# Counting and placing a graph's edges per block of source nodes: from broadcast rows with a scan to one-hot products with the edge on the partition

## The reference

```python
xt = jnp.einsum('nd,rde->rne', x, W)
agg = jax.ops.segment_sum(xt[rel, src], dst, num_segments=x.shape[0])
x = jax.nn.relu(agg + x @ SW + b)                     # twice
...
scores = jnp.einsum('ehd,ehd->eh', q[src], k[tgt]) / np.sqrt(HD) + (curv @ Wc + bc)
p = jnp.exp(scores - segment_max(scores, tgt)[tgt])
probs = p / segment_sum(p, tgt)[tgt]
out = jnp.zeros_like(x).at[src].add((probs[:, :, None] * v[tgt]).reshape(E, -1))
```

## Time and profile before

| | us |
|---|---|
| median of 3 runs | 9961.1 |
| lowest, highest | 9957.0, 10004.2 |
| the profiled execution, its own time | 10026.0 |
| its span | 10024.0 |
| POOL busy over the span | 6599.2 (66%) |
| DVE busy | 6480.5 (65%) |
| PE busy | 6317.1 (63%) |
| ACT busy | 2755.1 (27%) |

### The profile page before, as it was taken

One profiled execution on the slowest core, in us unless ns is written; L12 is line 12 of the kernel. 1 busy time (PEld: TensorE's weight loads), 2 busy tenths in 40 slices (PEclk: granted clock), 3 DMA queues, 4 the chain that ended last, 5 costly groups with the idle time before them and its releaser, 6 DMA issues. The chain is left out here.

```text
span 10024.0 us, 168284 instructions
## 1 busy us (share of the span) xinstructions
PE 6317.1 (63%) x28252; PEld 5567.6 (56%) x28253; DVE 6480.5 (65%) x17072; ACT 2755.1 (27%) x6953; POOL 6599.2 (66%) x6718
## 2 busy tenths in 40 slices
PE   0444444444676777767568888888735666666666
PEld 0233333333466666666448888888724565655555
DVE  6254444444566777766568888888864666666655
ACT  0100000000222222322135555555413333333301
POOL 1177777777377777777337777777647777777710
PEclk9755555555755555555565555555556777788757
DMA  1722222222322222222235555555424666666631
GB/s 29 216 62 62 62 62 62 62 62 62 140 58 55 61 60 60 61 55 59 57 100 137 137 137 137 137 137 137 117 60 117 147 150 149 146 151 151 150 91 30
DMA packets 1093415, 984.20 MB, mean 98 GB/s; under 512 B 224876, under 2 KB 970796, under 8 KB 1093243
## 3 DMA queue, kind: packets, MB, share of 16 engines
q0 software_dynamic: 214240, 442.60, 16.0%
q1 hardware_dynamic: 699363, 407.53, 15.4%
q10 hardware_dynamic: 179712, 133.04, 6.8%
HBM read 791.54 MB, written 210.74 MB: 100 GB/s over the span
## 5 line engine op out<-in xcount | busy, mean ns | idle before, releaser
L651 POOL DMA_INDIRECT stage_msg<-xt,stage_index x3328 | 3286.6, 988 | 1397.2 <-issue 1044.1
L673 PE MATMUL stage_ps_agg<-stage_hot,stage_msg 128*128 128x128 f32 x6656 | 1714.8, 439 | 1925.3 <-DMA stage_msg<-xt,stage_index 1761.0
L673 PEld LDWEIGHTS stage_ps_agg<-stage_hot,stage_msg 128*128 128x128 f32 x6656 | 1481.8, 328 | 2071.9 <-DMA stage_msg<-xt,stage_index 968.7
L1086 POOL DMA_INDIRECT big<-q,stage_index x1664 | 1587.3, 954 | 756.7 <-issue 488.4
L1474 POOL DMA_INDIRECT slots<-big,stage_index x1664 | 1681.3, 1010 | 530.8 <-issue 445.9
L746 DVE TENSOR_TENSOR big<-big,stage_ps_agg 128x128 f32 x3328 | 955.0, 287 | 1496.2 <-PE stage_ps_agg L673 1138.3
L620 ACT ACTIVATE stage_index<-big 128x4 int32 (+1 forms) x832 | 170.2, 205 | 2911.0 <-PE stage_ps_agg L673 2901.2
L1528 PE MATMUL stage_ps_sums<-stage_hot,big 128*128 128x128 f32 x4160 | 800.4, 361 | 182.0 <-DVE big L1646 174.1
L1518 PE MATMUL stage_ps_val<-nodes_a,big 128*128 x3328 | 665.1, 361 | 312.6 <-ACT big L1432 289.2
L1528 PEld LDWEIGHTS stage_ps_sums<-stage_hot,big 128*128 128x128 f32 x4160 | 728.8, 267 | 234.2 <-DVE big L1646 181.0
L1161 PE MATMUL stage_ps_key<-nodes_a,big 128*128 x3328 | 794.9, 414 | 0.0
(11 more groups left out here) (253 smaller groups left out, 8661.2 us busy)
## 6 DMA issues: line engine op xcount, KB each, us to landing
big<-slots SPq DMA_DIRECT2D x2080, 66.0 KB
big<-in_edge_attr_dram SPq DMA_DIRECT2D x1664, 64.0 KB
stage_trow<-targets ACTq DMA_DIRECT2D x832, 128.0 KB
xt<-big SPq DMA_DIRECT2D x26, 2048.0 KB, 6.6
stage_msg<-xt,stage_index POOLq DMA_INDIRECT x3328
stage_lanes<-buckets SPq DMA_DIRECT2D x832, 49.0 KB
big<-q,stage_index POOLq DMA_INDIRECT x1664
slots<-big,stage_index POOLq DMA_INDIRECT x1664
```

What stands on the lines that cost most here:

```text
L651: pool.indirect_dma_start(msg[q][:, j, :], None, xt, bass.IndirectOffsetOnAxis(ap=index[q][:, j:j + 1], axis=0))\
L673: last = nc.tensor.matmul(ps[q % 2][:, j, :], msg[q][:, j, :], hot[q % 2][:, j, :], start=True, stop=True)
L1086: pool.indirect_dma_start(qrow[q][:, j * D:(j + 1) * D], None, d["q"], bass.IndirectOffsetOnAxis(ap=index[q][:, j:j + 1], axis=0))\
```

## The change

- `prepare_edges` no longer makes `buckets`. Behind the transposes DVE makes `block` (source >> 7) from the transposed `source`, with the edge on the partition, and keeps it in SBUF in half precision.
- The broadcast rows, their DMAs on SP and the eight copies of the mark table go. `score` and `scatter` read the marks from `tile_marks` with the head as a dimension of stride zero.
- Both runs: DVE makes `block_hot`, a one-hot of 4 x 49 columns on 128 partitions, half precision, for group x+1, directly behind L723.
- First run: PE sums `block_hot` over the partitions and the four tiles by four half-precision products with one column of ones; ACT copies the result to `counts`, four groups later.
- Second run: DVE scales an identity by `begin` (`base`, 49 x 49). PE adds up in PSUM, for every edge and block, `begin` plus the earlier tiles' edges of the block plus the earlier edges of the tile: one single-precision product (196 columns) and four in half precision (147, 98, 49 and 196 columns). DVE multiplies that by `block_hot` and reduces over the blocks into `slot_of`. Scan, both ACT passes, ACT's copy and the four single-column products go.

```diff
         link(nc.vector.tensor_scalar(target[:, :, :], target[:, :, :], -1.0, None, ALU.add))
 
-        link(nc.vector.tensor_scalar(bucket, srow, 7, None, ALU.arith_shift_right))
-        link(nc.vector.tensor_copy(bucket16[:, :, :], bucket))
         link(nc.vector.tensor_scalar(penalty[:, :, :], valid[:, :, :], BIG, -BIG, ALU.mult, ALU.add))
...
+        v.wait_ge(s_cp, 2 * len(CH))
+        link(nc.vector.tensor_copy(block_i, t["source"][:, :]))
+        link(nc.vector.tensor_scalar(block_i, block_i, 7, None, ALU.arith_shift_right))
+        link(nc.vector.tensor_copy(t["block"][:, :], block_i))
...
+    CONST = 1 if first else 3
     block = m.stack.enter_context(nc.Block())
     xt = d["xt"].rearrange("n (r e) -> (n r) e", r=R)
 
-    @block.sync
-    def _(sp):
-
-        def group(x):
-            q = x.slot()
-            if x.live(-SLOTS):
-                sp.wait_ge(s_counted if first else s_own, x.at(-SLOTS) + 1)
-            sp.dma_start(lanes[q][:, :], d["buckets"][bass.ds(x.at() * (G * P), G * P)].partition_broadcast(W))\
-                .then_inc(s_lanes[q], 16)
-
-        if first:
-            for h in range(H):
-                sp.dma_start(d["marks"].rearrange("(k h) e -> k h e", h=H)[:, h, :], d["tile_marks"])\
-                    .then_inc(s_mk, 16)
-        walk(sp, group, 0, 0)
-        if first:
-            sp.wait_ge(s_mk, 16 * H)
-
...
+            if first and x.live(-SLOTS):
+                act.wait_ge(s_met, x.at(-SLOTS) + 1)
+                nc.scalar.activation(t["counts"][:, bass.ds(x.at(-SLOTS), 1)], ps_met[x.slot(-SLOTS, 2)][0:W, 0:1],
+                                     ACT.Copy).then_inc(s_counted, 1)
+
+        walk(act, group, 0, SLOTS if first else 0)
+        if first:
+            act.wait_ge(s_counted, GROUPS)
...
         def group(x):
             if x.live():
-                q = x.slot()
+                q, h = x.slot(), x.slot(0, 2)
                 pe.wait_ge(s_hot, x.at() + 1)
                 pe.wait_ge(s_read, x.at() + 1)
                 pe.wait_ge(s_msg[q], x.turn() * (16 * G) + (16 * G + at[q]))
                 for j in range(G):
-                    last = nc.tensor.matmul(ps[q % 2][:, j, :], msg[q][:, j, :], hot[q % 2][:, j, :],
+                    last = nc.tensor.matmul(ps[h][:, j, :], msg[q][:, j, :], hot[h][:, j, :],
                                             start=True, stop=True)
                 last.then_inc(s_freed, 1)
-            if not first and x.live(-2):
-
-                h = x.slot(-2, 2)
-                pe.wait_ge(s_pick, x.at(-2) + 1)
-                if x.live(-4):
-                    pe.wait_ge(s_kept, x.at(-4) + 1)
-                for j in range(G):
-                    last = nc.tensor.matmul(ps_slot[h][:, j:j + 1], pick[h][:, j * P:(j + 1) * P], one[:, :],
-                                            start=True, stop=True)
-                last.then_inc(s_slot, 1)
-
-        walk(pe, group, 0, 0 if first else 2)
+                pe.wait_ge(s_block_hot, x.at() + 1)
+                if first:
+                    if x.live(-2):
+                        pe.wait_ge(s_counted, x.at(-2) + 1)
+                    for j in range(G):
+                        last = nc.tensor.matmul(ps_met[h][0:W, 0:1], block_hot[h][:, j, :], ones16[:, 0:1],
+                                                start=(j == 0), stop=(j == G - 1))
+                    last.then_inc(s_met, 1)
+                else:
+                    pe.wait_ge(s_base, x.at() + 1)
+                    if x.live(-2):
+                        pe.wait_ge(s_pick, x.at(-2) + 1)
+                    rank = ps_rank[h][:, 0:G * W].rearrange("p (j w) -> p j w", w=W)
+                    nc.tensor.matmul(rank, ones[:, 0:P], base[h][:, :].unsqueeze(1).to_broadcast([W, G, W]),
+                                     start=True, stop=False)
+                    for j in range(G - 1):
+                        nc.tensor.matmul(rank[:, j + 1:G, :], ones16[:, :],
+                                         block_hot[h][:, j, :].unsqueeze(1).to_broadcast([P, G - 1 - j, W]),
+                                         start=False, stop=False)
+                    nc.tensor.matmul(rank, earlier[:, :], block_hot[h][:, :, :], start=False, stop=True)\
+                        .then_inc(s_rank, 1)
+
+        walk(pe, group, 0, 0)
 
     @block.vector
     def _(v):
         v.sem_inc(s_read, 2)
+        nc.vector.memset(ones16[:, :], 1.0).then_inc(s_const, 1)
         if not first:
...
         def group(x):
             if x.live(1):
+                h = x.slot(1, 2)
+                here = bass.ds(x.at(1) * G, G)
 
                 v.wait_ge(s_freed, x.at(1) + SLOTS - 1)
                 nc.vector.tensor_tensor(
-                    hot[x.slot(1, 2)][:, :, :], t["iota16"][:, :].unsqueeze(1).to_broadcast([P, G, P]),
-                    t["target"][:, bass.ds(x.at(1) * G, G)].unsqueeze(2).to_broadcast([P, G, P]),
-                    ALU.is_equal).then_inc(s_hot, 1)
-            if x.live():
-                h, q = x.slot(0, 2), x.slot()
-                if first:
-                    v.wait_ge(s_lanes[q], x.turn() * 16 + 16)
-                    if x.live(-1):
-                        v.wait_ge(s_counted, x.at())
-                    nc.vector.tensor_scalar(met[h][:, :], lanes[q][:, :], t["lane"][0:W, :], 0.0, ALU.is_equal,
-                                            ALU.add, accum_out=t["counts"][:, bass.ds(x.at(), 1)])\
-                        .then_inc(s_counted, 1)
...
-                else:
-                    v.wait_ge(s_own, x.at() + 1)
-                    if x.live(-2):
-                        v.wait_ge(s_pick, x.at(-2) + 1)
-                    nc.vector.tensor_tensor_scan(run[h][:, :], ones[:, :], own[h][:, :],
-                                                 begin[:, bass.ds(x.at(), 1)], ALU.mult, ALU.add).then_inc(s_run, 1)
+                    hot[h][:, :, :], t["iota16"][:, :].unsqueeze(1).to_broadcast([P, G, P]),
+                    t["target"][:, here].unsqueeze(2).to_broadcast([P, G, P]), ALU.is_equal).then_inc(s_hot, 1)
+                if x.live(-1):
+                    v.wait_ge(s_met if first else s_rank, x.at(-1) + 1)
+                    if not first:
+                        v.wait_ge(s_pick, x.at(-1) + 1)
+                nc.vector.tensor_tensor(
+                    block_hot[h][:, :, :], t["iota16"][:, 0:W].unsqueeze(1).to_broadcast([P, G, W]),
+                    t["block"][:, here].unsqueeze(2).to_broadcast([P, G, W]), ALU.is_equal).then_inc(s_block_hot, 1)
+                if not first:
+                    nc.vector.tensor_scalar(base[h][:, :], t["ident"][0:W, 0:W], begin[:, bass.ds(x.at(1), 1)], None,
+                                            ALU.mult).then_inc(s_base, 1)
+            if x.live():
                 w = offsets(nc, mybir.EngineType.DVE, t["window"], x.at() * G, G)
                 v.wait_ge(s_freed, x.at() + SLOTS + 1)
                 for j in range(G):
...
                     v.wait_ge(s_acc, x.at() * G + j + 1)
                 v.sem_inc(s_read, 1)
                 if not first:
-                    v.wait_ge(s_run, x.at() + 1)
-                    if x.live(-2):
-                        v.wait_ge(s_slot, x.at(-2) + 1)
-                    nc.vector.tensor_tensor(pick[h][:, :], run[h][:, :], own[h][:, :], ALU.mult)\
-                        .then_inc(s_pick, 1)
+                    h = x.slot(0, 2)
+                    v.wait_ge(s_rank, x.at() + 1)
+                    if x.live(-1):
+                        v.wait_ge(s_kept, x.at())
+                    nc.vector.tensor_tensor(pick[:, :, :], ps_rank[h][:, 0:G * W].rearrange("p (j w) -> p j w", w=W),
+                                            block_hot[h][:, :, :], ALU.mult).then_inc(s_pick, 1)
+                    v.wait_ge(s_pick, x.at() + 1)
+                    nc.vector.tensor_reduce(t["slot_of"][:, bass.ds(x.at() * G, G)], pick[:, :, :], AX.X, ALU.add)\
+                        .then_inc(s_kept, 1)
 
         walk(v, group, 1, 0)
-        if first:
-            v.wait_ge(s_counted, GROUPS)
+        if not first:
+            v.wait_ge(s_kept, GROUPS)
...
+def marks_of(d, group, a, b):
+
+    return d["tile_marks"][bass.ds(group * G, G), a:b].unsqueeze(1).to_broadcast([G, H, b - a])
...
                     sp.wait_ge(s_tot, x.at(-4 - SLOTS) + 1)
-                sp.dma_start(mark[q][:, :], d["marks"][bass.ds(x.at(-4) * GH, GH), 0:2 * (P + 1)])\
-                    .then_inc(s_mk[q], 16)
+                sp.dma_start(mark[q][:, :], marks_of(d, x.at(-4), 0, 2 * (P + 1))).then_inc(s_mk[q], 16)
             if x.live():
```

74 lines of the change are left out of this document (23 added, 51 removed).

## The result

After takes 9912.24 us (median of 10 runs, 9905.71 to 9920.79), before, on the same chip, 9973.22 (10 runs, 9950.36 to 10017.44): a ratio of 0.9919, 95% interval 0.9889 to 0.9948, so 0.8% faster. The forecast was 9970, from a sum that made the change 9 us slower. The profiled run of after took 9909.68 us with a span of 9907.7, against 10026.0 and 10024.0: 116 us less.

The account below looks back on a forecast made before the run. POOL, issuing gathers without a pause, was taken as the bound. Terms -59 - 3 + 54 + 17 = +9 gave 10035 against the profiled run, 9970 after a 65 us offset to the median; 8-in-10 range 9845 to 10045.

Parts of the forecast that it names:

- The standstill: POOL's 59.5 us stop after its first 24 gathers, DVE waiting for a broadcast row behind the mark copies; goes: -59 us.
- The preparation: Ahead of the transposes, two DVE operations and one store leave the path: -3 us.
- f: L723's start after a group's first gather, in us: 0.42 or 0.78 in the first aggregation, 1.13 in the second after the change.
- the chain: L723 and the new 196-column product directly behind it, in both aggregations, taken to hold a gather as one until the second ends.
- H: Length of the chain from L723's start: 0.97 us after the change, 0.68 before in the first aggregation.
- the first aggregation: Gather stretch per group there grows from 0.036 to 0.16 us over 416 groups: +54 us, ends 0 to +95.
- the second: Second aggregation: mean gather stretch per group 0.36 us against 0.32 before, over 416 groups: +17 us.
- X: Stretch of a gather that starts while the chain runs: f + H - 1.375 if positive; mean 0.36 us in the second aggregation.
- (b): Half-precision product doesn't hold POOL, or holds it for less, in both aggregations: -104 us (9857) or -55 (9906); chance 0.16.
- (a): Second aggregation: L723 slips behind the second gather and stretches none, total -141 us, 9820; chance 0.20.
- (c): More short DVE work, such as the scaling step, holds POOL in both aggregations: +79 us, 10040; chance 0.16.
- (d): POOL's standstill in the first aggregation isn't removed by the change: +68 us, 10029; chance 0.03.

Follow-up runs that it names:

- e7: Before with only the eight copies of the mark table gone, marks read from the small table with stride zero: 9938.38 us, ratio to before 0.9936.
- e13: After with the eight mark copies made again and read in the score and scatter stages: 9922.01 us, ratio to before 0.9915.
- e14: After itself, unchanged, run as a control beside before: 9919.99 us, ratio to before 0.9931.
- e8: After with a plain 512-column product directly ahead of hot, on 49 partitions in the first aggregation, 128 in the second: 10108.67 us (one execution).
- e3: After with block_hot in single precision in the first aggregation and hot made twice in the second: 12343.29 us, ratio to before 1.0034.
- e1: Before with only the eight copies of the mark table gone, in the 12.3 ms condition: 12380.24 us, ratio to before 1.0064.
- e2: After with the row of numbers for both one-hot products read from PSUM, in the 12.3 ms condition: 12325.75 us, ratio to before 1.0021.
- e5: After with the row of numbers for both one-hot products read from PSUM, in the 10 ms condition: 9809.99 us, ratio to before 0.9803.
- e12: After with the numbers in PSUM, and the scatter stage's one-hot product made as five comparisons, 10 ms condition: 9769.95 us, ratio to before 0.9770.
- e10: After with plain 49-partition products: one between hot and block_hot in the first aggregation, two ahead of hot in the second: 12347.54 us (one execution, 12.3 ms condition).
- e4: After with the second aggregation's reduction made twice, so hot starts 0.36 us later, in the 12.3 ms condition: 12319.98 us, ratio to before 1.0018.
- e11: After with the numbers in PSUM, and the scatter stage's one-hot product made as five comparisons, 12.3 ms condition: 12357.04 us, ratio to before 1.0047.

## Why the prediction was wrong

*What held.* POOL is the bound and issues without a pause (gap 0.305 in the aggregations of every kernel of the 10 ms condition). The standstill: -59 forecast, -57.6 with the stage's +1.9 in it, and e7 and e13 show its cause. The preparation gave 6.0 for 3. The work taken from ACT and the scan bought nothing: the stretches of the second aggregation add up to 131 us in before and 92 in after, and that is all of the 38.8. hot starts 2.71 us after the end of its group's matmuls in the second aggregation, as put together beforehand, so f = 1.13 stood; the placing products on PE took 1.54 us together (1.02 single, 0.52 more for the four half-precision ones), 1.4 forecast. The marks, taken as 0 with ends of 12, were -8 in the profiled runs and -3 in e13 against e14.

*The step that failed* is the chain, "so the chain is H = 0.61 + 0.36 = 0.97 us instead of 0.68": the overlap of a gather with two products taken as one. The sentence ahead of it, "It has two SBUF inputs, so I let it hold as L723 does", is right as it stands: L709 does hold, for gathers that begin during it. But I read two back-to-back products as one chain, from the earlier trace rows, where L754 passes its gather on to L723. That is a special case: e8 shows it for a product on 49 partitions ahead of hot and not for the same one on 128; e3 shows that two of the very kind of L723 don't chain. Between two products of 128 partitions a waiting gather gets through. So H was 0.68. That mis-sizes both terms: the first aggregation, +54 forecast, gave +1.9; the second, +17 forecast with X = 0.36, has X = (1.13 + 0.68 - 1.375)/2 = 0.22, and the row gives 4 x (0.999 - 0.944) = 0.22: -38.8. So the sum had the wrong sign. These are rival (b)'s numbers, by another mechanism than (b) named: not that the half-precision product doesn't hold, but that holding isn't handed over; that (b) came nearest is luck.

*The sign that I had in hand and misread* is in the earlier trace rows: the scan L740 follows L723 without a pause and the gather doesn't wait for it. I took it for a property of the scan, "shows no such effect", and rested (b) on it. The scan does hold. In before no gather could show it: 440 began during L740, 27 of them within 0.01 us of its start and the others in its last 0.08. In e1, where the scan is L734, POOL's pauses put some in its middle:

```profile
4476.72 1.27 DVE L734 TENSOR_TENSOR_SCAN stage_run<-stage_ones,stage_begin,stage_own 49x512 f32<-49x512 bf16 x1
...
4476.94 1.81 POOL L645 DMA_INDIRECT stage_msg<-xt,stage_index  x1 [2.06 <-issue]
```

That gather took 0.87 us over 0.944 and was let go 0.19 before the scan's end; the same holds for all 7 gathers of e1 that began 0.20 to 0.99 us into a scan. In the score stage of after 157 gathers that began during one of its four scans of 32 partitions were stretched in the same way. So the earlier trace rows already showed two holding instructions back to back with a gather let through between them, the very case that the chain denied.

*A second step failed,* the passage from the profiled run to the median. I took the 65 us between them over to after; by it the measured terms would have given about 9845. But after's profiled run stands at its median (9909.7 and 9912.2) and its 10 runs lie within 15 us, before's 10 within 67. The likely reason that the profiled run of before stood high is its second aggregation: chains that began just ahead of a gather and held it for up to 1.1 us, 83 times, by way of the narrow L754. In after the longest stretch in that stage is 0.52. e7, with before's placing work, spreads as widely (78 us), and in this stage its trace differs from before's in just these chains. No trace of an execution of before near its median was taken, so this part is argued and not shown. So by the medians the change brings less than by the traces: the mark copies alone gave 50 (9988.3 to 9938.4), and after 71 beside e14 (9990.8 to 9920.0); the new placing is worth some 20 by the difference, which the intervals (40 us either way for e7, 25 for e14) don't tell from nothing or from the 39 of the traces.

*Range and rivals.* The time lay within 9845 to 10045, outside the forecast's own 9930 to 10010. Rivals (a), (c) and (d) are excluded: 356 gathers began during hot in the second aggregation, so it didn't slip past them; the scaling step holds nothing (76 gathers of e2 began during it there, 65 of them where a hold would have shown as 0.08 us or more, and none was stretched by more than 0.01); and POOL has no gap.

*The page rule.* The Trainium skill, "GPSIMD Engine Reference", section 8 (Key points), says that GpSimd and VectorE contend where a VectorE instruction has two SBUF inputs. e5 agrees (one input moved to PSUM: 0.946 for 0.954 and 0.999), and so do the scans of e1 and of the score stage, which the prediction took for an exception. The comparisons of e12 have one tensor and one number per partition in SBUF and hold too; whether they run in a two-port mode no row here shows (128 columns in a step of 0.20, 32 columns of a two-input product in 0.19).

## What to carry to other kernels

Where POOL issues indirect DMAs without a pause, look at which DVE products with two SBUF operands run when one starts: here moving a row of 128 numbers to PSUM was worth 101 us by the traces, cutting a long product into five shorter ones 40, and 0.36 us of added work at the right place 91. Before pricing two effects as one chain, find rows in which the same two kinds follow each other, and take every case in the trace that speaks against the chain as evidence and not as an exception. Where the executions of a kernel spread widely, find out which stage spreads before an offset between profile and median is carried over to the changed kernel.

## What the runs showed that I had not expected

*A hold has sharp edges.* A product of 0.69 us holds a gather that starts from 0.05 us after the product's start on and lets it go 0.125 before its end (0.56 after the start). Products with one operand in PSUM (60 gathers that began well inside L729 of after), reductions (103 in e2), the comparison L733 of 49 x 512 half-precision numbers (306 in before) and the scaling of 49 x 49 numbers hold none. Products and scans of two SBUF tensors, and comparisons of 128 x 128 single-precision numbers with one per partition, do, each for itself; a scan lets go 0.19 before its end.

*49 partitions and 128 differ* in passing a held gather on, at equal durations (e8, e10); the reason stays open.

*The same kernel at 9988 and at 12297 us on one chip.* In the 12.3 ms condition POOL's idle time on indices grows; the two rows are before without copies, first e1, then e7. Below them a pause of e2 in order of time:

```profile
L645 POOL DMA_INDIRECT stage_msg<-xt,stage_index x3328 | 3355.0, 1008 | 2024.7 <-issue 1127.3 <-ACT stage_index L614 897.4
...
L645 POOL DMA_INDIRECT stage_msg<-xt,stage_index x3328 | 3313.9, 996 | 1336.3 <-issue 1047.3 <-ACT stage_index L614 289.0
```

```profile
1498.27 0.94 POOL L619 DMA_INDIRECT stage_msg<-xt,stage_index  x1 [0.30 <-issue]
...
1500.26 0.36 DVE L713 TENSOR_TENSOR stage_block_hot<-stage_ps_iota,block 128x196 bf16<-128x196 f32 x1 [4.29 <-remote]
...
1502.51 0.20 ACT L600 ACTIVATE stage_index<-big 128x4 int32 x1 [2.09 <-remote]
...
1503.52 0.94 POOL L619 DMA_INDIRECT stage_msg<-xt,stage_index  x1 [4.30 <-ACT stage_index L600]
```

DVE had its operands and stood 4.29 us before L713, ACT 2.09 before the index; a register instruction of DVE took 0.70 us on either side of that wait, where the same ones take 0.04 to 0.08 in e5. Once in a loop of four groups POOL then stands some 4 us, and 20.1 us a loop become 24. That DVE and ACT came late by their instructions is my reading; the trace names only "remote". In that condition shorter gathers showed in no time (e2 without any stretch took 12325.75, e4 with its stretches 12319.98), DVE's load counted (e11), and the kernels with strided mark reads were slower than before (1.0018 to 1.0064) while the one with copied marks was faster (0.9901): its score stage took 2950 us for 3031 in e2, its scatter stage 2814 for 2882. Which of two kernels is faster can thus depend on the condition; after itself was not run in it.
